# Windowed attention: the values products of a tile in one block, ten places for transposed pairs, a 128-row stationary operand for the spreading

## What is computed

```python
q = (x @ Wq).reshape(B, S, H, hd)
k = (kv_latent @ Wk).reshape(B, S, H, hd)
v = (kv_latent @ Wv).reshape(B, S, H, hd)
mask = (ki <= qi) & ((qi - ki < WINDOW) | (ki < PERSIST))   # 128 and 16
scores = jnp.einsum('bqhd,bkhd->bhqk', q, k) * scale
scores = jnp.where(mask[None, None], scores, jnp.finfo(scores.dtype).min)
attn = jax.nn.softmax(scores, axis=-1)
out = jnp.einsum('bhqk,bkhd->bqhd', attn, v).reshape(B, S, D)
return out @ Wo
```

## Time and profile before

| | us |
|---|---|
| median of 3 runs | 4574.59 |
| lowest, highest | 4567.81, 4588.4 |
| the profiled execution | 4576.1 |
| its span, first to last instruction | 4574.2 |
| TensorE busy in the span | 4213.9 (92%) |
| DVE busy | 2097.7 (46%) |
| ACT busy | 1663.7 (36%) |
| attention stage of the first layer, about 385 to 951 | 566 |

### The profile page before, as it was taken

How to read it: one execution, slowest core, us unless ns; L and a number is a source line. 1 busy time by engine, 2 the same in 40 slices (tenths; PEclk the granted TensorE clock), 3 DMA queues, 4 the chain that set the end, 5 groups by cost and what they waited for, 6 DMA issues and landing times. The chain is left out here.

```text
span 4574.2 us, 68643 instructions
## 1 busy us (share of the span) xinstructions
PE 4213.9 (92%) x23045; PEld 3557.8 (78%) x23046; DVE 2097.7 (46%) x4006; ACT 1663.7 (36%) x3234; POOL 1220.5 (27%) x1809
## 2 busy tenths in 40 slices
PE   6966888879999999999997999998799999999998
PEld 5854667668989888888886777776578888788887
DVE  4457666644444444444444554453333333333333
ACT  2214766643343434343332333332222222222222
POOL 0012444434444444444442233333100000000000
PEclk8877999989999999999998999998899999999999
DMA  5776666635555556565554443342423222221221
GB/s 199 284 231 162 128 136 128 114 96 118 113 126 120 130 112 130 114 131 118 124 116 130 168 150 121 133 134 71 143 76 104 97 87 75 97 99 63 97 81 48
DMA packets 351750, 560.87 MB, mean 123 GB/s; under 512 B 33057, under 2 KB 198593, under 8 KB 347330
## 3 DMA queue, kind: packets, MB, share of 16 engines
q1 hardware_dynamic: 282770, 394.19, 29.3%
q0 software_dynamic: 68784, 164.10, 16.9%
HBM read 383.84 MB, written 174.34 MB: 122 GB/s over the span
## 5 line engine op out<-in xcount | busy, mean ns | idle before, releaser
L1206 POOL DMA_INDIRECT acc_d<-e_yw,e_to x208 | 336.1, 1616 | 342.4 <-ACT e_yw L1339 330.6
L2244 POOL DMA_DIRECT2D out<-d_res x32 | 17.3, 542 | 1305.3 <-DVE d_res L2476 1305.3
L2423 DVE TENSOR_TENSOR d_h<-d_sg,d_psU 128x512 f32<-128x512 f32 x144 | 99.1, 688 | 520.1 <-PE d_psU L107 461.7
L972 ACT ACTIVATE a_pr<-a_sm,a_nmax 128x272 f32<-128x272 f32 x512 | 264.0, 516 | 164.3 <-DVE a_nmax L1027 122.5
L105 PE MATMUL e_psG<-e_gu,e_xT 128*128 128x352 f32 x832 | 286.3, 344 | 8.5 <-DVE e_xT L1393 8.5
L1401 DVE TENSOR_TENSOR e_h<-e_sg,e_psU 128x352 f32<-128x352 f32 x208 | 108.4, 521 | 387.3 <-ACT e_sg L1352 383.9
L1027 DVE CUSTOM_DVE_ANT_0 a_sm<-a_psS,a_mask 128x272 f32<-128x272 f32 x512 | 213.1, 432 | 156.7 <-PE a_psS L867 134.8
L107 PE MATMUL e_psU<-e_gu,e_xT 128*128 128x352 f32 x832 | 268.8, 323 | 0.0
L105 PE MATMUL e_psU<-e_gu,e_xT 128*128 128x352 f32 x832 | 268.5, 323 | 0.0
L106 PE MATMUL e_psU<-e_gu,e_xT 128*128 128x352 f32 x832 | 268.3, 323 | 0.0
L106 PE MATMUL e_psG<-e_gu,e_xT 128*128 128x352 f32 x832 | 267.8, 322 | 0.0
(11 more groups left out here) (423 smaller groups left out, 11901.8 us busy)
## 6 DMA issues: line engine op xcount, KB each, us to landing
d_gu_raw<-in_wgu SPq DMA_DIRECT2D x144, 512.0 KB, 3.2
qk_d<-f_qk SPq DMA_DIRECT2D x32, 1024.0 KB
a_q<-qk_d SPq DMA_DIRECT2D x96, 256.0 KB
a_k<-qk_d SPq DMA_DIRECT2D x96, 256.0 KB
e_rawgu<-in_w_gate SPq DMA_DIRECT2D x32, 704.0 KB
e_rawgu<-in_w_up SPq DMA_DIRECT2D x32, 704.0 KB
b_gu_raw<-in_wgu SPq DMA_DIRECT2D x40, 512.0 KB, 3.9
xT_d<-f_xT SPq DMA_DIRECT2D x16, 1024.0 KB
```

Source lines behind the costliest of these rows:

```text
L972: act.activation(pr[half][:, h % HH, :], sm[s % SR][:, :], ACT.Exp, bias=nmax[s % SR][:, :], scale=-1.0, accum_out=rs[u % 2][:, h:h + 1]). ...
L1206: pool.indirect_dma_start(env.acc_d, bass.IndirectOffsetOnAxis(ap=to[:, :].bitcast(U32), axis=0), yw[:, :], None, compute_op=ALU.add).then ...
L2423: ins = dve.tensor_tensor(hv[q % 2][:, :], sg[q % 2][:, :], psU[:, :], ALU.mult)
```

## The change

Four edits in `phase_attend`.

- `values` for all four groups of a tile is issued in one block in step `NH - 1 + LAG` = 20 after the tile's first head. Before, the groups stood in steps 8, 12, 16 and 20.
- `TR`, the places for transposed pairs, goes from 8 to 10. The wait of the copies is written anew in `slot_free`: a copy waits for the group that used the pair ten pairs earlier.
- `sel` gets 128 partitions instead of 16 (rows past 16 are zero), and the spreading's matmuls run over 128 rows of `xT`.
- What follows moves: spreading from step 19 to 21, persistent values and `inverse_out` from 20 to 22, division from 21 to 23, cast and subtraction from 22 to 24, projection from 25..28 to 26..29, copy to `y` from 29 to 30.

```diff
-    TR = 8
+    TR = 10
...
-        sel = sb("a_sel", [NH, NGR, GH, HD])
+        sel = sb("a_sel", [P, NGR, GH, HD])
...
+        def slot_free(eng, u, p):
+
+            i = u * HH + p - TR
+            if i >= 0:
+                eng.wait_ge(pv_done, i // HH * NGR + i % HH // 2 + 1)
+
...
                     ins = pe.matmul(psR[:, g, :], sel[:, g, :, :].rearrange("p j d -> p (j d)"),
-                                    xT[u % 2][0:NH, 2 * P:3 * P], start=True, stop=True)
+                                    xT[u % 2][:, 2 * P:3 * P], start=True, stop=True)
...
-                for g in range(NGR):
-                    if (u := tile_of(s, GH * g + GH - 1 + LAG)) is not None:
+
+                if (u := tile_of(s, NH - 1 + LAG)) is not None:
+                    for g in range(NGR):
                         values(u, g)
                 if (u := tile_of(s, X_AT)) is not None:
                     turn_sums(u)
-                if (u := tile_of(s, X_AT + 2)) is not None:
+                if (u := tile_of(s, X_AT + 4)) is not None:
                     spread(u)
-                if (u := tile_of(s, X_AT + 3)) is not None:
+                if (u := tile_of(s, X_AT + 5)) is not None:
                     pers_values(u)
                 for c in range(KC):
-                    if (u := tile_of(s, X_AT + 8 + c)) is not None:
+                    if (u := tile_of(s, X_AT + 9 + c)) is not None:
                         project(u, c)
...
-                    if u:
-                        act.wait_ge(pv_done, (u - 1) * NGR + p // 2 + 1)
+                    slot_free(act, u, p)
...
-                if (u := tile_of(s, X_AT + 3)) is not None:
+                if (u := tile_of(s, X_AT + 5)) is not None:
                     inverse_out(u)
-                if (u := tile_of(s, X_AT + 5)) is not None:
+                if (u := tile_of(s, X_AT + 7)) is not None:
                     out_hi(u)
...
-                    if u:
-                        dve.wait_ge(pv_done, (u - 1) * NGR + p // 2 + 1)
+                    slot_free(dve, u, p)
...
-                if (u := tile_of(s, X_AT + 4)) is not None:
+                if (u := tile_of(s, X_AT + 6)) is not None:
                     divide(u)
-                if (u := tile_of(s, X_AT + 5)) is not None:
+                if (u := tile_of(s, X_AT + 7)) is not None:
                     out_lo(u)
-                if (u := tile_of(s, X_AT + 12)) is not None:
+                if (u := tile_of(s, X_AT + 13)) is not None:
                     finish(u)
```

## The result

| | before | after |
|---|---|---|
| median, us (7 runs each, same chip) | 4579.22 | 4561.84 |
| lowest, highest | 4567.81, 4588.4 | 4555.99, 4567.05 |
| the profiled execution | 4576.1 | 4567.05 |
| first to last spreading, a tile | 17.31 | 16.97 |

The ratio is 0.9963, interval 0.9949 to 0.9977: 17.4 us less, 0.37%, faster but within half a per cent. The forecast was 4548, 27 us less (it is counted from the three runs of before that were then on record, median 4574.59). The profiled executions differ by 9 us, because that of after is the longest of its seven.

A forecast was written before the change was run, and what follows sets the result against it. The prediction held that TensorE, though busiest, waits 3.4 us a tile on the score, DVE, ACT and turning loop. A tile of 16.45 against 17.31 saves 27 us: 4576.1 - 27 + 0.5 - 1.5 = 4548, range 4508 to 4590, its own 4530 to 4562.

The forecast's parts named there:

- The walk of the new tile: Attention stage: one tile of the new order followed in four stretches from the first projection, 16.45 us against 17.31.
- 1, projection to sums: First projection to sums: projection steps, then reduction, exponential, turn and four transposes, 5.94 us.
- 2, sums to block: Sums to the merged values block: TensorE waits for ACT's copy of the sums and an exponential, 2.63 us.
- 3, block to persistent values: Merged block of 64 (1.88 us), score, transposes, spreading and score up to the persistent values, 3.58 us.
- 4, to the projection: Persistent values through reduction, division and cast to the next projection: 4.02 to 4.54 us, taken as 4.3.
- two: Behind a values block that a score follows, TensorE's signals come late, at most 1.5 us (first block), 2.4 (third).
- One, changes of shape: TensorE's array-shape changes cost busy time: 0.33 us per values block, 0.3 for the 16-row spreading.
- TensorE is the bound: Rival, chance 0.15: TensorE sets the pace, so all 2.4 us a tile come off, 75 us, giving 4501.
- The lag stays with the block: Rival, chance 0.25: late signals persist behind the merged block; 2.4 us makes a tile 17.5, about 4581, no change.
- The term of 2.4 us: Size of signal lag behind the merged block in the lag rival; it would add 1.1 us a tile.
- Slower: Rival, chance 0.10: the lag grows with the block; at 3.3 us a tile takes 18.4, giving 4609.
- The parts at no cost: Copies waiting on ten places cost zero, key loads stay covered; first-block and spreading waits, 17.4 and 18.9 us, go.

The follow-up runs named there:

- before_scatter_late: The kernel before with POOL's 192 indirect stores issued behind its loop instead of in it; 4802.06 us in all, 16.41 us a tile in the stage.
- after_16_rows: The changed kernel with the spreading's stationary operand back at 16 rows; 4565.81 us, ratio to before 1.0041.
- pad_again: The kernel before with only the 128-row operand added, run on the third chip; 4571.85 us, ratio 0.9967.
- after_third: The changed kernel, unchanged, run on the third chip; 4566.10 us, ratio to before 0.9954.
- before_again: The kernel before, unchanged, traced on the second chip; 4595.78 us in one run, 17.81 us a tile.
- after_again: The changed kernel, unchanged, run on the second chip; 4566.95 us, ratio to before 0.9956.
- pad_alone: The kernel before with only the 128-row operand added, run on the first chip; 4527.27 us, ratio 0.9963.
- moves_without_block: The changed kernel with the four values groups back in steps 8, 12, 16 and 20, first chip; 4523.24 us, ratio to before 0.9948.
- chain_first: The changed kernel with division, cast and subtraction ahead of DVE's and ACT's other work in step 23, first chip; 4521.15 us, ratio to before 0.9952.
- chain_first_two_blocks: The changed kernel with division, cast, subtraction put first and values in two blocks (steps 16 and 20), second chip; 4540.88 us, ratio to before 0.9903.

## Why the prediction was half right

The direction was right, the size was not: 17 us came in place of 27. 4561.84 lies in the range and at the very end of the forecast's own, 4562. That the direction came out right is in part luck, as the subtraction below shows.

**The walk of the new tile.** Against the undisturbed tiles of after:

| step | forecast | measured |
|---|---|---|
| 1, projection to sums | 5.94 | 6.26 |
| 2, sums to block | 2.63 | 2.41 |
| 3, block to persistent values | 3.58 | 3.58 |
| 4, to the projection | 4.3 | 4.21 |
| sum | 16.45 | 16.46 |

Step 3 was exact (644.08 to 647.66). Step 1 was too small: I had priced a projection behind a turned pair like one behind a score, but its first product stands 0.32, not 0.24, ahead of the next (653.66 to 653.98, against 654.57 to 654.81). That and the like 0.31 behind a wait (652.39 to 652.70) are 0.23 of the 0.32. Step 2 was too large by about as much. So the sum agrees partly by luck.

**The step that failed is the subtraction of the walk from 17.31.** The walk has neither late signals nor dips of the clock; the 17.31 has both. I had seen the late signals ("two"), but wrote them to the values block, so I let them go with it: the forecast took before as it was, after as if undisturbed. Like with like it is 16.46 against 16.47, nothing. By parts: 16.46, less 0.38 for the padding (16.08), less 0.15 for the later steps and ten places (15.93), plus 0.54 for the merging (16.47).

The sizes under "two" were too large as well. Ahead of 604.64 DVE had been idle for 0.34, so there a late signal cost at most that. Behind the third block DVE starts 2.21 behind the score's start (610.97 to 613.18), in before_scatter_late 0.93 (601.83 to 602.76): 1.3 later.

The new tile is subject to both disturbances too. The stations of its trace split 16.97 up:
- 16.47 undisturbed, as in the period from 578.16.
- Late pair copy: 17 of 31 tiles have 4.65 to 4.74 in place of 4.21 from persistent values to projection: 17 x 0.48 / 31 = 0.26.
- Clock: six tiles hold a stretch of half clock, each 1.4 to 1.6 longer: 0.30 a tile, 9 us.
- The last period is 2.5 shorter (-0.08), and three more have 0.15 to 0.4 extra (0.02).

Before, by the same count, 17.31 is 16.41 (the mean of before_scatter_late, with its shorter last period) + 0.24 for six dips, which lengthen the stations ahead of the first projection by 7.4 us in all, and 0.66 that is left for late signals. (Where a dip falls, the last station has 1.5 to 1.8 in place of 2.3: behind a dip the late signals cost less. So those six tiles are only 4.1 us longer than others.) After has 16.41 + 0.30 + 0.26. So the measured gain of 0.34 a tile is 0.40 less for late signals, less 0.06 more for the clock. The late signals now fall behind the persistent values, beside a wait for the chain, and no longer behind the sums, where the spreading waited for them. That is argued from the traces of both. Its test in the other direction is after_16_rows: on the chip without late signals the change, there without its padding, loses 0.41%, 18.6 us by the ratio and 22.6 by the medians. After itself wasn't run there; taking off the padding's 12 (stations) to 16 us (medians), I estimate 3 to 11 us slower than before on such a chip. The intervals of the two runs are some 7 us wide on either side, so that no difference is not ruled out.

**One, changes of shape.** Right for the padding. The Trainium skill (TensorEngine Tiling (Array Packing), Key Properties) has a change of tiling mode drain TensorE; the trace agrees in that the 16-row operand beside the 128-row one costs 0.30 from the spreading on and 0.1 ahead of it. But 0.33 for each of three values blocks that were merged away is time of TensorE that nobody waited for in the first of them and in part of the others.

**Rivals.** "TensorE is the bound": fell. 34 us of busy time went and 17 us of time, and the padding by itself gave 16 on the first chip and 18 on the third. On neither is the rest of the change shown to add to that: pad_again has 0.9967 and after_third 0.9954, with intervals that overlap. "The lag stays with the block": a lag there is, but not behind the block. DVE starts at 646.51 on a score that ends at 646.36. The term of 2.4 us did not come; POOL's three stores now run from 1.0 to 4.5 us behind the block's end (647.04 to 650.57), and the signal that is late is that of the pair at 648.70. "Slower": no.

**The parts at no cost.** Ten places: no wait of a copy for a place shows in the waits view, as said, and none for the key loads. The waits of 17.4 and 18.9 us are gone; the prediction's "late next is the values block" holds for the spreading (0 wait).

**The chain.** I listed ACT's additional exponential (4.02 to 4.54), but not that the pair copy stands there too, at 649.90. It is this copy through which the late signal reaches the projection: 4.7 instead of 4.2.

## The clock

In the windows view the granted clock of after's tiles is 1.00 or 0.91. An undisturbed period, one with a dip, and the middle of that dip:

```profile
407.36:423.77 16.41, 13.86 (x146) 11.95 (x144) 11.50 (x42) 12.13 (x38) 7.70 (x16) 1.00 0.64 130
423.77:441.81 18.04, 15.46 (x145) 13.25 (x144) 11.50 (x42) 12.23 (x38) 7.37 (x13) 0.91 0.62 118
430.00:433.00 3.00, 3.00 (x12) 2.60 (x11) 0.78 (x5) 1.71 (x5) 0.00 (x0) 0.50 1.26 183
```

The clock falls to its lower level, 1.2 GHz, for about 3.4 us. In after each of the six dips begins between 0.4 us ahead of the start of the first projection and 0.7 us behind it, where TensorE had waited 62.6 / 31 = 2.0 us on average. The projection steps run through it, and the tile grows by 1.4 to 1.6. Before has six dips as well, but they begin 1.6 to 2.6 us behind the start of a spreading, and the six tiles grow by 4 us together. Other traces of the same kernels have other counts: before_again 15 dips, after_again three, after_third six. pad_alone, pad_again, moves_without_block, before_scatter_late and chain_first show none between the first and the last spreading. chain_first has 0.89 us of wait ahead of the projection, not 2.25, which may be why it has none; that wasn't tested by itself. For it speaks that chain_first_two_blocks, with the chain in the same order on another chip, has no dip at the projection; but it has three some 7.6 us ahead of one, each with a tile 1.2 to 1.8 longer. Why before has dips and pad_again has none stays open.

## What to carry to other kernels

Before merging small groups on a busy engine, look at what the engine does where each group stands: one that fills a wait is free there, and in a block it can cost in full, as here. When a forecast subtracts a walked-through tile from a measured one, make both of the same kind: list the disturbances in the measured one (late starts, clock dips) and ask where each falls in the new order. When an idle engine starts late on finished work, look at all engines in that stretch, above all at DMAs issued by POOL, and not only at the instruction ahead.

## What was not expected of the hardware

- Signals of TensorE reach DVE and ACT late while POOL issues indirect stores or just behind them (0.96 us each, three in a row): the copy of the sums starts up to 2.82 us behind them in pad_again, 2.0 more than in pad_alone. So it is in the traces of the chips of the result and of the second and third group; never in the four traces of the first chip, with the same stores. It would explain most of why before takes 4543 us there and 4588 elsewhere: with the clock's part, (17.31 to 17.81 less 16.41) x 31 = 28 to 43. Before has no trace on the first chip, so this is argued. Why one chip is free of it stays open, and so does how the stores do it.
- A stationary operand of 16 rows costs 0.38 us more a visit than the same operand padded with zeros to 128, although the trace shows the spreading's eight records as 1.15 us in the one and 1.06 in the other.
